# Weighted sums ahead of transposes, and the first layer norm by groups of 512 tokens

## What is computed

```python
def _layernorm(x, axis=-1, eps=1e-05):
    m = jnp.mean(x, axis=axis, keepdims=True)
    v = jnp.var(x, axis=axis, keepdims=True)
    return (x - m) / jnp.sqrt(v + eps)

xn = _layernorm(x, axis=-1)
s = _L0_attn_ref(xn, ...)      # a state space block: 16 states, conv of 4 taps, softplus, scan
g = _silu(_L0_ffn_ref(xn, ...))
x = x + s * g

# _L0_ffn_ref: six layers of local attention (16 heads of 64, windows of 32) and a gated MLP
for i in range(DEPTH):
    x = attn_layer(shift_tokens(x), Wqkv[i], q_scale[i], k_scale[i], Wo[i]) + x
    x = ffn_layer(shift_tokens(x), ln_g[i], ln_b[i], W1[i], b1[i], W2[i], b2[i]) + x
```

## Time and profile before

| | |
|---|---|
| median of 3 runs | 3765.09 us (3764.43 to 3771.79) |
| the profiled execution, its own time | 3770.5 us |
| its span | 3768.7 us |
| PE busy | 3501.3 us, 93% |
| weight loads | 2248.3 us, 60% |
| DVE busy | 3257.1 us, 86% |
| ACT busy | 3031.0 us, 80% |
| POOL busy | 2918.3 us, 77% |
| granted TensorE clock, mean | 0.983 |

### The profile page before, as it was taken

The page is one execution under the profiler, slowest core; times in us unless marked ns, Lnnn a source line. Parts: engine busy times, 40 slices in busy tenths (PEclk is TensorE's granted clock), DMA queues, the critical chain, the costliest instruction groups (busy, mean ns, idle before and its releaser), DMA issues.

```text
span 3768.7 us, 95852 instructions
## 1 busy us (share of the span) xinstructions
PE 3501.3 (93%) x31040; PEld 2248.3 (60%) x31040; DVE 3257.1 (86%) x11659; ACT 3031.0 (80%) x8795; POOL 2918.3 (77%) x2417
## 2 busy tenths in 40 slices
PE   5898699999999999999999999999999999999997
PEld 2454366666666666666666666666666665666664
DVE  5778598988988988889889889889898899888985
ACT  3556488888888888888888888888888888888886
POOL 3878587787887878878878778788788788787783
PEclk9899799999999999999999999999999999999999
DMA  2000232323332333323233333233232233332322
GB/s 74 15 6 9 89 113 95 108 102 109 116 103 100 105 103 114 109 98 107 101 105 115 107 101 106 99 112 111 100 110 102 100 116 104 109 105 98 105 100 85
DMA packets 239965, 364.17 MB, mean 97 GB/s; under 512 B 43278, under 2 KB 80204, under 8 KB 239372
## 3 DMA queue, kind: packets, MB, share of 16 engines
q1 hardware_dynamic: 239468, 358.05, 28.1%
HBM read 125.93 MB, written 5.77 MB: 35 GB/s over the span
## 4 chain that ended last, share of the span: by engine, by line
PE 59%; DVE 18%; POOL 8%; issue 8%; ACT 5%; DMA 2%; SPq 1%; DVEq 0%; POOLq 0%; ACTq 0%
PE bank L736 9%; PE bank L725 7%; PE bank L328 6%; DVE ab L1301 6%; PE bank L697 5%; PE bank L330 5%; PE bank L329 5%; PE bank L679 4%; PE bank L764 4%; DVE sm L1346 4%; PE bank L706 3%; PE bank L707 3%; POOL pr L1086 2%; POOL rot L1094 2%; DVE pt L1333 2%
## 5 line engine op out<-in xcount | busy, mean ns | idle before, releaser
L937 ACT ACTIVATE pr<-sm,nb,rq 128x128 f32<-128x128 f32 (+1 forms) x3072 | 1517.4, 501 | 28.5 <-DVE nb L1352 28.5
L1086 POOL TENSOR_TENSOR pr<-pr,rden 128x640 f32<-128x640 f32 x768 | 964.8, 1256 | 512.6 <-DVE rden L1326 511.1
L1301 DVE TENSOR_TENSOR ab<-bank,ltab 128x512 f32<-128x512 f32 x1536 | 985.5, 683 | 183.8 <-PE bank L330 166.0
L1094 POOL TENSOR_TENSOR rot<-ab,swp 128x512 f32<-128x512 f32 x768 | 985.9, 1284 | 100.5 <-DMA swp<-ab 98.4
L1346 DVE CUSTOM_DVE_ANT_0 sm<-bank,mask 128x128 f32<-128x128 f32 (+1 forms) x3072 | 840.9, 330 | 38.0 <-PE bank L697 35.3
L937 ACT ACTIVATION_READ_ACCUMULATOR pr<-sm,nb,rq 128x1 f32 x3072 | 598.6, 195 | 0.0
L697 PEld LDWEIGHTS bank<-rot 64*64 64x64 f32 x12288 | 288.3, 132 | 430.7 <-issue 351.8
L1100 POOL TENSOR_TENSOR rot<-rot,rkb 128x512 f32<-128x512 f32 x384 | 491.7, 1287 | 64.5 <-DMA rkb<-k_scratch 64.2
L1333 DVE COPY pt<-bank 128x512 f32<-128x512 f32 x768 | 531.4, 692 | 10.2
L925 ACT ACTIVATE sq<-bank 128x512 f32<-128x512 f32 x768 | 451.5, 588 | 55.1 <-DVE ab L1301 48.7
L697 PE MATMUL bank<-rot 64*64 64x96 f32 x12288 | 432.0, 256 | 56.2 <-DVE nb L1352 32.9
(11 more groups left out here) (204 smaller groups left out, 6382.4 us busy)
## 6 DMA issues: line engine op xcount, KB each, us to landing
swp<-ab SPq DMA_DIRECT2D x1536, 128.0 KB, 2.0
rkb<-k_scratch SPq DMA_DIRECT2D x768, 128.0 KB, 2.9
xs<-xT SPq DMA_DIRECT2D x95, 128.0 KB, 2.3
xs<-xT SPq DMA_DIRECT2D x95, 127.5 KB, 2.4
raw<-Wqkv SPq DMA_DIRECT2D x48, 128.0 KB, 2.5
raw<-Wqkv SPq DMA_DIRECT2D x12, 256.0 KB, 2.9
wo<-Wo SPq DMA_DIRECT2D x6, 512.0 KB, 4.9
k_scratch<-rsum SPq DMA_DIRECT2D x192, 8.0 KB
```

The lines of the kernel that those rows point to most:

```text
L937: ins = act.activation(pr[:, s % 4, i, t, 0:P + WINDOW * t], sm[:, s % 2, i, cs], ACT.Exp, bias=nb[:, s, t, i:i + 1], scale=head_scale(rq, ...
L1086: ins = pool.tensor_tensor(pr[:, e % 4, :, :, :], pr[:, e % 4, :, :, :], rden[:, e, :, :].rearrange("p t i -> p i t").unsqueeze(3) .to_bro ...
L1094: pool.tensor_tensor(rot[:, PAIRS * (j % 2) + j // 2, :], ab[:, j % 2, 0, :], swp[:, j % 2, :], ALU.add).then_inc(qk_rot, 1)
L1301: ins = dve.tensor_tensor(seqs(ab[:, j % 2, i, :]), seqs(use_bank("qk", j)[:, :]), ltab[:, 2 * (j % 2) + i:2 * (j % 2) + i + 1, :] .to_bro ...
```

## The change

- In the flow, PE's `outputs` stands ahead of `transpose_probs` in a step.
- x comes in eight transfers, one for each group, into pt and pr, which the flow uses later. The order is x of group 0, the taps and five other constants (`consts_in`, 6 transfers), x of group 1, five later constants (`later_in`), x of groups 2 to 7.
- The layer norm goes by groups. DVE sums 4 tiles and scales by -1/128; ACT squares each tile with the mean as bias and accumulates, one tile after the other through one scratch tile, makes the reciprocal root, and scales and shifts each tile in one activation; DVE makes the shift as a product over 4 columns. PE transposes four tiles into bank 3, ACT copies the bank to xT.
- Groups 0 and 1 are done in front: group 0 ahead of the first convolution, group 1's transposes behind it, its copy between silu and `xd`. Group g+2 is done inside state space group g (six times), at the steps of LN_AT.
- `statepick` is gone: the picks are written from columns of ident with a step of zero.
- `dt` waits for the copy of g+2's group to xT, for both use bank 3.

```diff
@@ -41,6 +41,7 @@
 STATE_PE = {0: (0,), 1: (1,), 2: (2,), 3: (3, 4), 7: (5, 6, 7, 'xdbl'), 12: ('dt',)}
 STATE_ACT = {7: ('silu',), 10: ('xd',), 13: ('soft',)}
 STATE_DVE = {11: ('xlow',), 13: ('relu',)}
+LN_AT = {"square": 3, "rstd": 5, "normal": 8, "sum": 1, "shift": 7, "turn": 11, "store": 12}
 STATE_AT = {'skip': 3, 'out': 5, 'out_sb': 6, 'delta': 13}
 EARLY = 5
@@ -358,14 +355,24 @@
 
         @block.sync
         def _(sp_e):
-            sp_e.dma_start(xtok, x_in.rearrange("b (t p) c -> p (b t) c", p=P)).then_inc(xtok_in, 16)
-            for dst, src in ((ident[:, :], ident_c), (w_in, W_in), (mv[:, :], mvec),
-                             (w_xdbl, W_xdbl), (w_dt[0:DT_RANK, :], W_dt),
-                             (w_out[:, :].rearrange("p (t c) -> p t c", t=2), W_out.rearrange("(t p) c -> p t c", p=P)),
-                             (statepick[0:96, :, :], statepick_c), (lv_all[:, :], lvec),
-                             (tab[:, :, :], tabs_c), (mask[:, :], mask_c), (headsum[:, :, :], headsum_c),
-                             (taps_c, conv_w[:, :].to_broadcast([P, D_CONV * 2 * P]).rearrange("p (k n) -> p k n", k=D_CONV))):
+            xv = x_in.rearrange("b (t p) c -> p (b t) c", p=P)
+
+            def load_x(g):
+
+                sp_e.dma_start(xtok[g], xv[:, 4 * g:4 * g + 4, :]).then_inc(x_tok[g], 16)
+
+            load_x(0)
+            for dst, src in ((w_in, W_in),
+                             (taps_c, conv_w[:, :].to_broadcast([P, D_CONV * 2 * P]).rearrange("p (k n) -> p k n", k=D_CONV)),
+                             (ident[:, :], ident_c), (mv[:, :], mvec), (w_xdbl, W_xdbl), (w_dt[0:DT_RANK, :], W_dt)):
                 sp_e.dma_start(dst, src).then_inc(consts_in, 16)
+            load_x(1)
+            for dst, src in ((w_out[:, :].rearrange("p (t c) -> p t c", t=2), W_out.rearrange("(t p) c -> p t c", p=P)),
+                             (lv_all[:, :], lvec), (tab[:, :, :], tabs_c), (mask[:, :], mask_c),
+                             (headsum[:, :, :], headsum_c)):
+                sp_e.dma_start(dst, src).then_inc(later_in, 16)
+            for g in range(2, GROUPS):
+                load_x(g)
 
             def load_chunk(layer, c):
@@ -512,15 +518,16 @@
         @block.tensor
         def _(pe):
 
-            pe.wait_ge(consts_in, 16 * NCONST)
-            pe.wait_ge(ln0_xn, 1)
-            for t in range(TILES):
-                if t >= 16 and t % 4 == 0:
-                    pe.wait_ge(ln0_xT, t // 4 - 3)
-                mm = pe.transpose(bank[t // 4 % 4][:, t % 4 * P:t % 4 * P + P], xtok[:, t, :], ident[:, :])
-                if t % 4 == 3:
-                    mm.then_inc(ln0_tr, 1)
-            pe.wait_ge(ln0_xT, GROUPS)
+            def turn_x(g):
+
+                after(pe, m_soft, g - 1, 1, 0)
+                after(pe, m_rl, g - 1, 1, 0)
+                if g > 0:
+                    pe.wait_ge(ln0_xT, g)
+                pe.wait_ge(ln0_xn, 4 * g + 4)
+                for t in range(4):
+                    mm = pe.transpose(bank[3][:, t * P:t * P + P], xtok[g][:, t, :], ident[:, :])
+                mm.then_inc(ln0_tr, 1)
 
             def prelude(part, g, par):
 
@@ -528,6 +535,8 @@
                     src = seqs(xT[:, bass.ds(g * GT, GT)])
                     i, piece = part // 4, part % 4
                     k, lo, hi = ((1, 0, SEQ), (0, 1, SEQ), (2, 0, SEQ - 1), (3, 0, SEQ - 2))[piece]
+                    if part == 0:
+                        pe.wait_ge(ln0_xT, g + 1)
                     if piece == 0:
                         after(pe, m_silu, g, 2, i - 1)
                     mm = pe.matmul(seqs(bank[i][:, :])[:, :, lo:hi], w_conv[:, k, i * P:i * P + P],
@@ -544,6 +553,7 @@
                     after(pe, m_xd, g, 1, 1)
                     after(pe, m_soft, g, 1, 0)
                     after(pe, m_rl, g, 1, 0)
+                    pe.wait_ge(ln0_xT, min(g + 2, GROUPS))
                     pe.matmul(bank[3][:, :], w_dt[0:DT_RANK, :], xd[0:DT_RANK, :], start=True, stop=True)\
                         .then_inc(m_dt, 1)
 
@@ -590,13 +600,22 @@
                         add_pair(n // 2 + 6, before)
                     if n == STATE_AT["out"] and g > 0:
                         state_out(before, 1 - par)
+                    if n == LN_AT["turn"] and g + 2 < GROUPS:
+                        turn_x(g + 2)
                     if more:
                         for part in STATE_PE.get(n, ()):
                             prelude(part, following, 1 - par)
 
+            pe.wait_ge(consts_in, 16 * NEARLY)
+            turn_x(0)
+            pe.wait_ge(conv_made, 1)
+            for part in range(8):
+                prelude(part, 0, 0)
+            turn_x(1)
+            for part in ("xdbl", "dt"):
+                prelude(part, 0, 0)
             pe.wait_ge(consts_made, 1)
-            for part in (*range(8), "xdbl", "dt"):
-                prelude(part, 0, 0)
+            pe.wait_ge(later_in, 16 * NLATER)
             state_groups(pe, group)
             for k in (6, 7):
@@ -798,14 +817,14 @@
                             down(c, group_of(role, o))
                     if AT["wo"] <= s < AT["wo"] + NWO and prev is not None:
                         project_out(s - AT["wo"], prev)
+                    if s % 2 == 0 and s < 6 and prev is not None:
+                        outputs(s, s // 2 + 5, prev)
+                    if s % 2 == 0 and s >= 6 and cur is not None:
+                        outputs(s, s // 2 - 3, cur)
                     if s < 3 and prev is not None:
                         transpose_probs(s + 13, prev)
                     if s >= 3 and cur is not None:
                         transpose_probs(s - 3, cur)
-                    if s % 2 == 0 and s < 6 and prev is not None:
-                        outputs(s, s // 2 + 5, prev)
-                    if s % 2 == 0 and s >= 6 and cur is not None:
-                        outputs(s, s // 2 - 3, cur)
                     if s in V_STEPS and group_of(V_STEPS[s][0], o) is not None:
                         make_v(s)
@@ -825,15 +844,44 @@
         @block.scalar
         def _(act):
 
-            act.wait_ge(ln0_mean, 1)
-            act.activation(xsq, xtok, ACT.Square).then_inc(ln0_sq, 1)
-            act.wait_ge(ln0_var, 1)
-            act.activation(st[:, 2, :], st[:, 1, :], ACT.Ln).then_inc(link["act"], 1)
-            act.wait_ge(link["act"], 1)
-            act.activation(st[:, 3, :], st[:, 2, :], ACT.Exp, scale=-0.5).then_inc(ln0_rstd, 1)
-
-            act.wait_ge(consts_in, 16 * NCONST)
+            def x_squares(g, tiles):
+
+                act.wait_ge(ln0_mean, g + 1)
+                for t in tiles:
+                    if 4 * g + t > 0:
+                        act.wait_ge(ln0_sq, 4 * g + t)
+                    act.activation(xsq, xtok[g][:, t, :], ACT.Square, bias=st[g][:, 1, t:t + 1],
+                                   accum_out=st[g][:, 2, t:t + 1]).then_inc(ln0_sq, 1)
+
+            def x_rstd(g):
+
+                act.wait_ge(ln0_sq, 4 * g + 4)
+                act.activation(st[g][:, 3, :], st[g][:, 2, :], ACT.Ln, scale=1.0 / DIM, bias=eps[:, 0:1]).then_inc(ln0_ln, 1)
+                act.wait_ge(ln0_ln, g + 1)
+                act.activation(st[g][:, 4, :], st[g][:, 3, :], ACT.Exp, scale=-0.5).then_inc(ln0_rstd, 1)
+
+            def x_normal(g, tiles):
+
+                act.wait_ge(ln0_shift, g + 1)
+                for t in tiles:
+                    act.activation(xtok[g][:, t, :], xtok[g][:, t, :], ACT.Identity, scale=st[g][:, 4, t:t + 1],
+                                   bias=st[g][:, 5, t:t + 1]).then_inc(ln0_xn, 1)
+
+            def x_store(g):
+
+                act.wait_ge(ln0_tr, g + 1)
+                act.activation(xT[:, g * GT:g * GT + GT], bank[3][:, :], ACT.Copy).then_inc(ln0_xT, 1)
+
+            act.preload_act_table_set("natural_log_exp_and_others")
+            for g in range(2):
+                x_squares(g, range(4))
+                x_rstd(g)
+                x_normal(g, range(4))
+                if g == 0:
+                    x_store(0)
+            act.wait_ge(consts_in, 16 * NEARLY)
             act.wait_ge(consts_made, 1)
+
             def prelude(part, g, par):
 
@@ -894,13 +942,24 @@
                     act.activation(cC[n % NC], bank[5][:, :], ACT.Copy).then_inc(m_cc, 1)
                     if n == STATE_AT["out_sb"] and g > 0:
                         state_out(before)
+                    if g + 2 < GROUPS:
+                        if n in (LN_AT["square"], LN_AT["square"] + 1):
+                            x_squares(g + 2, ((0, 1), (2, 3))[n - LN_AT["square"]])
+                        if n == LN_AT["rstd"]:
+                            x_rstd(g + 2)
+                        if n in (LN_AT["normal"], LN_AT["normal"] + 1):
+                            x_normal(g + 2, ((0, 1), (2, 3))[n - LN_AT["normal"]])
+                        if n == LN_AT["store"]:
+                            x_store(g + 2)
                     if more:
```

(57 more changed lines are left out.)

31 lines of the change are left out of this document (11 added, 20 removed).

## The result

The changed kernel takes **3716.28 us** (median of 4 runs, 3715.8 to 3719.63) against 3768.44 (3764.43 to 3772.04, 4 runs) for the kernel before: a ratio of 0.9862, 95% interval 0.9847 to 0.9878. The profiled execution took 3719.63 with a span of 3717.8; spans are 50.9 apart.

What follows compares the result with a forecast made beforehand. Took PE to lead, DVE from step 10 of the state groups, and a serial front. Profiled 3770.5 - 33.7 (front) + 3 (groups) + 0 (flow) = 3739.8; against the runs 3765.1 - 30.7 = 3734.4 us, range 3722 to 3748.

Steps and rivals of the forecast that it cites:

- I take 0 for the flow: Flow, even steps: sums ahead of transposes change nothing in total, between -23 and +15 us.
- can remove the wait ahead of the transposes: Flow: PE's wait for DVE's copy of the probabilities, 0.24 us in step 10 and 0.50 in step 12.
- the 0.3 that the prediction named as a sign of being wrong: Flow: the prediction is wrong if a turn differs by over 0.3 us.
- the flow gains: Flow: step 12's 0.50 us isn't asked back in step 14, total 3711 us; chance 0.10.
- The front: Start to first convolution: it starts at 11.3 in place of 45.85, 34.5 us gained, 0.8 charged, so -33.7.
- not double: Front, picks widened from ident: 2.7 us in all, 4.3 if DVE goes at half rate; covered, by little.
- The groups: Six state space groups with the norm inside: +0.5 us each, +3 in all, bounds 0 to +10.
- The wait that was named: State groups: dt matmul waits for the copy to xT, delaying softplus and DVE's line 1211; +0.5 us a group.
- The split of x costs: Front: eight transfers each pay 2.6 us in turn, first convolution at 17, total 3740 us; chance 0.08.
- Late transposes: Flow: later transposes meet DVE's full stretch, step 8 named; slower than before, 3788 us at 1.13 a turn; chance 0.04.

Runs made afterwards that it cites:

- the split's step 6: Kernel before with half of the weighted sums ahead of the transposes and half behind, in even steps 0 to 8: 3829.18 us against 3770.84, ratio 1.0161.

## Why the prediction was wrong

**The term that failed is the flow: "I take 0 for the flow".** Its working looked for waits alone. It said that the change "can remove the wait ahead of the transposes", followed that wait through steps 10, 12 and 14, and found it asked back. That part held: step 10 waits 0.60 for the values and grows by 0.18 (forecast 0.32), step 12's wait goes, steps 13 and 14 take it back, and with the order changed there alone the kernel stays at -1.2 us by the runs and the undisturbed turn at -0.11. What it took for granted is that PE's own work costs the same in another order. It doesn't: one change of tile less in a step is 0.15 to 0.19 us less of busy time, step 6 had one too many, and 0.19 x 48 is 9 us. Steps 0, 2, 4 and 8 add 0.04 to 0.05 us each in undisturbed turns, 8 to 9 us in 48 turns. The rows to see it in were there, and I read none of them: behind scores, four transposes take 0.41 us ahead of a projection and 0.59 ahead of the sums, in the trace of the kernel before. The mean turn changed by 0.35 us, over the 0.3 that the prediction named as a sign of being wrong.

The rival "the flow gains" named the right total (3711 for step 12's 0.50 kept, and 3716 came) by a mechanism that the runs refute: step 12's wait was asked back, as the forecast had it. The range didn't reach so far, since that rival had only a tenth of the chance.

**The front** held within 1.3 us: 34.67 gained at the first convolution (34.5 forecast) and 2.2 given back up to the last scan of the first group (0.8 charged), 0.7 of it by the first product and 1.5 in the scans behind it. Its terms: x used from 3.73 (4.2 taken); squares 0.53 each (0.6); four scalings 1.65, so 0.41 each (0.3 taken). For the scalings the Trainium skill (ScalarE: Activation LUTs, Rules for kernel authors) was right with 0.41, where I scaled the trace's 0.23 for a tiny tile too low. The picks cost 0.68 for 1024 columns, as in the earlier trace rows, not double, and stayed covered. That the convolution started within 0.12 us of the 11.3 forecast is in part luck: x and the squares came some 0.8 us early together, the scalings with their hand-over 0.6 late.

**The groups** cost 0 rather than 3: a period of 40.96 us, where 41.4 was forecast. The wait that was named came: dt waits 0.41 for the copy to xT, and DVE waits 1.96 ahead of line 1272 where it waited 1.13, 0.8 a group. It comes back behind the group's end. There the granted clock is at its lower level for a while; by stretch, in the changed kernel, where the next convolution starts at 195.21:

```profile
194.00:195.00 1.00, 1.00 (x2) 0.34 (x1) 0.87 (x2) 0.86 (x2) 0.92 (x2) 0.50 0.00 0
195.00:196.00 1.00, 1.00 (x2) 0.34 (x1) 1.00 (x2) 0.00 (x0) 1.00 (x2) 0.50 0.00 0
196.00:198.00 2.00, 2.00 (x7) 1.28 (x6) 1.21 (x3) 0.15 (x1) 0.61 (x1) 0.87 0.00 0
```

and in the kernel before, where it starts at 227.77:

```profile
226.00:228.00 2.00, 2.00 (x4) 0.90 (x3) 1.87 (x3) 1.11 (x2) 1.92 (x3) 0.50 0.00 0
...
229.00:230.00 1.00, 1.00 (x3) 0.43 (x2) 0.00 (x0) 0.00 (x0) 0.17 (x1) 0.50 0.00 0
230.00:231.00 1.00, 1.00 (x5) 0.77 (x4) 0.43 (x1) 0.00 (x0) 0.00 (x0) 0.63 0.00 0
```

The half clock (1.2 GHz) reached some 2.9 us into the convolution and the next group's first steps; now it ends 1.3 us after their start. That is 1.6 us less at half speed, or 0.8 us of work, as much as the wait had cost. This reading agrees with the rows, and no run tested it.

**The other rivals.** The split of x costs: no, x of group 0 is there at 3.73, and the other pieces of x take a median of 4.6 to 5.4 us to landing with several under way, not one after the other; the advice to coalesce that the prediction cites (the Trainium skill, DMA: Bandwidth & Descriptors, Rules for kernel authors) doesn't bind at 256 KB here. Late transposes: no; DVE waits longer for them, but in steps 2 to 5 alone, and step 8 is shorter. That mechanism did show in another form, in step 8 of the kernel with the sums right behind the scores, with ACT in DVE's place and 0.16 us.

**Left open.** By the runs steps 0 to 8 alone give 12 us, 10 to 14 alone 1.2, both together 17.9; by undisturbed turns it would be 17, 5 and 22. What is missing lies in the turns at the layers' borders, which vary from execution to execution, and in the stages ahead: kernels with the same first two stages reach the first scores of the flow anywhere between 435.5 and 444.1 us in their profiled executions, and the kernel before itself ran from 3759 to 3775. Nor does every change cost the same. Ahead of the sums it is 0.17 behind transposes and 0.09 behind projections or centring (from 0.96 to 1.06 us for the centring); behind a narrow tile the transposes take 0.06 more and a projection 0.02. That is why steps 0, 2, 4 and 8 gain 0.04 to 0.05 us with three changes in both orders, and why 0.15 to 0.19 holds for leaving out a visit to the full width, not for each border. Scores take 0.49 us whether sums or transposes follow. The 0.15 us of the split's step 6 could also be the price of starting a second burst of sums, as all of it shows in the sums; what the change itself saves can't be that, since it starts as many. A change of tile by itself, with no other work around it, wasn't run.

## What to carry to other kernels

On an engine that is busy all the time, the order of its own instructions has a price, not only the waits between engines: count how often the tile changes in a step and put work of equal tiles side by side, first where the engine never waits, then look for who now gets its input later. Before costing a reorder at nothing, compare the time that the same instructions take beside different neighbours; what differs belongs to the place, not to the work. And a serial stage is cheapest where something slower runs beside it, even in a form that is dearer by itself.

## What the runs showed of the hardware

- Changes between the tiles 64\*64, 128\*64 and 128\*128 cost PE time: step 6 takes 3.90, 4.09 and 4.24 us with two, three and four changes, and splitting the sums in five steps of a turn costs 58 us in all. The profile counts it as busy.
- At a change of tile the first weight load starts with its matmul (a median lead of 0.002 us in the flow); between transposes and projections, which share a tile, it starts 0.03 us ahead.
- A cast from a source with a zero step takes as long as one from a dense source: 0.68 us for 96x1024 either way.
- A transfer of 256 KB, the first to be issued, is used 3.73 us into the span, where the one of 2 MB was at 10.93.
- ACT's square of 128x128 with its accumulator read repeats every 0.53 us when each waits for the one before; a scaling of 128x128 every 0.41.
